# Tensor-product layer of a graph network: ScalarE scales the weights in place in PSUM, and VectorE's products read them there

## The reference, cut to what matters

```
h = silu(edge_attr @ fc_w1 * 8**-0.5)
h = silu(h @ fc_w2 * 64**-0.5)
wA, wB, wC, wD = split(h @ fc_w3 * 64**-0.5, 4)
es, ev = ys[dst], yv[dst]                 # 64 scalars, 64 x 3 vectors
sh0, sh1 = edge_sh[:, :1], edge_sh[:, 1:] # 1 and 3 numbers per edge
m0a = wA * es * sh0
m0b = wD * einsum('eud,ed->eu', ev, sh1) / sqrt(3)
m1a = wB[:, :, None] * es[:, :, None] * sh1[:, None, :]
m1b = wC[:, :, None] * ev * sh0[:, :, None]
ns, nv = segment_sum(concat(m0a, m0b), src), segment_sum(concat(m1a, m1b), src)
```

## Time and profile before

| | |
|---|---|
| Time of 3 runs | 9382.79, 9408.56, 9411.95 us; median 9408.56 |
| Profiled execution, span from first to last instruction | 9608.8 us (its device time is not recorded apart) |
| Stretch of the tensor-product layer's edge loop | from about 4396 to 5876 us |
| Busy in that stretch of 1480 us | PE 1424.10, DVE 1297.62, POOL 1179.54, ACT 451.01 us |
| TensorE's granted clock in that stretch | 0.99 of full speed |

### The profile page before, as it was taken

One profiled execution on the slowest core, in us unless ns is written; L12 is line 12 of the kernel. 1 busy time (PEld: TensorE's weight loads), 2 busy tenths in 40 slices (PEclk: granted clock), 3 DMA queues, 4 the chain that ended last, 5 costly groups with the idle time before them and its releaser, 6 DMA issues. The chain is left out here.

```text
span 9608.8 us, 121761 instructions
## 1 busy us (share of the span) xinstructions
PE 6035.1 (63%) x27004; PEld 3698.3 (38%) x27227; DVE 5624.6 (59%) x14481; ACT 2416.0 (25%) x7255; POOL 5956.5 (62%) x5564
## 2 busy tenths in 40 slices
PE   2121155555555555547999997899999997554544
PEld 0010033333333333334444444555555555333333
DVE  4100055555555555556888887899999998222224
ACT  0000033333333333322333332344444443000000
POOL 5777655555555555546888884566666665666663
PEclk6555566666666666668999998999999999667676
DMA  1000032223222232322332333344444444333334
GB/s 64 1 10 10 17 88 83 83 78 83 81 80 80 81 83 78 81 55 73 85 84 85 84 84 52 111 120 119 119 119 121 120 119 101 90 90 89 89 90 55
DMA packets 405871, 777.59 MB, mean 81 GB/s; under 512 B 195938, under 2 KB 225356, under 8 KB 405196
## 3 DMA queue, kind: packets, MB, share of 16 engines
q0 software_dynamic: 279488, 712.60, 28.4%
q1 hardware_dynamic: 126348, 64.59, 2.3%
HBM read 736.75 MB, written 40.07 MB: 81 GB/s over the span
## 5 line engine op out<-in xcount | busy, mean ns | idle before, releaser
L495 POOL DMA_INDIRECT rec_s<-wts,rows x784 | 780.5, 995 | 1085.2 <-ACT rows L467 870.5
L1829 POOL DMA_INDIRECT gat<-y,rec_sb_s x892 | 1182.5, 1326 | 298.0 <-issue 278.8
L2098 POOL DMA_INDIRECT gat<-x,rec_sb_d x892 | 846.5, 949 | 484.5 <-issue 266.2
L965 POOL DMA_INDIRECT gat<-kv,rec_sb_d x896 | 906.7, 1012 | 334.7 <-issue 272.9
L1381 POOL DMA_INDIRECT gat<-kv,rec_sb_s x900 | 861.5, 957 | 398.5 <-issue 313.9
L2113 PE MATMUL ps<-gat,oh 128*128 128x256 f32 x1760 | 648.5, 538 | 680.2 <-DVE acc L2133 253.6
L1577 DVE TENSOR_REDUCE small<-ps 128x2 f32<-128x1024 f32 x884 | 1041.7, 1216 | 6.9 <-PE ps L1445 5.7
L434 POOL DMA_INDIRECT rec_d<-small x784 | 810.7, 1034 | 343.0 <-issue 265.1
L1870 PE MATMUL ps<-big,oh 128*128 128x512 f32 x1760 | 947.3, 637 | 0.0
L2113 PEld LDWEIGHTS ps<-gat,oh 128*128 128x128 f32 x1760 | 462.9, 274 | 865.5 <-issue 497.1
L1048 PE MATMUL ps<-big,oh 128*128 128x264 f32 x1768 | 754.1, 541 | 0.3
(11 more groups left out here) (276 smaller groups left out, 13129.7 us busy)
## 6 DMA issues: line engine op xcount, KB each, us to landing
gat<-kv,rec_sb_s POOLq DMA_INDIRECT x900
gat<-kv,rec_sb_d POOLq DMA_INDIRECT x896
rec_sb_s<-rec_s SPq DMA_DIRECT2D x448, 32.0 KB, 2.2
gat<-y,rec_sb_s POOLq DMA_INDIRECT x892
gat<-x,rec_sb_d POOLq DMA_INDIRECT x892
rec_d<-small POOLq DMA_INDIRECT x784
rec_s<-wts,rows POOLq DMA_INDIRECT x784
rec_s<-gat SPq DMA_DIRECT2D x4, 1808.0 KB, 16.7
```

The lines of the kernel that those rows point to most:

```text
L495: e.indirect_dma_start(out=recs["s"], out_offset=bass.IndirectOffsetOnAxis(ap=pr[:, t:t + 1], axis=0), in_=rr[:, t, :], in_offset=None).th ...
L965: e.indirect_dma_start(out=gat[:, m.u, q, :], out_offset=None, in_=table, in_offset=bass.IndirectOffsetOnAxis(ap=r_sb[:, m.u, q, 0:1].bitc ...
L1829: e.indirect_dma_start(out=rows_y[m.u][:, q, :], out_offset=None, in_=y1, in_offset=bass.IndirectOffsetOnAxis(ap=r_sb[:, m.u, q, 0:1].bitc ...
L2098: e.indirect_dma_start(out=gat[:, m.u, q, 0:D], out_offset=None, in_=x3, in_offset=bass.IndirectOffsetOnAxis(ap=r_sb[:, m.u, q, 0:1].bitca ...
```

## The change

The tile `wac`, in which ACT put the scaled `wA` and `wC`, was a piece of the SBUF tile `work`. It is now another name for the places of `wA` and `wC` in `psW` itself. ACT's four activations read and write the same addresses in PSUM, and DVE's L1941 and L1942 take their weights from PSUM in place of SBUF. No semaphore, no count and no order of instructions is changed on any engine.

```diff
             h2 = work[:, 384:640]
-            wac = work[:, 1536:2048].rearrange("p (q a n) -> p q a n", q=Q, a=2)
             wb = work[:, 2048:2304].rearrange("p (q n) -> p q n", q=Q)
...
             psW = ps[:, 3:5, :].rearrange("p b c -> p (b c)").rearrange("p (q k n) -> p q k n", q=Q, k=4)
+            wac = psW[:, :, 0:3:2, :]
...
                 for q in range(Q):
-                    last = A.activation(wac[:, q], psW[:, q, 0:3:2, :], ACT.Copy, scale=r_sb[:, m.u, q, 2:3])
+                    last = A.activation(wac[:, q], wac[:, q], ACT.Copy, scale=r_sb[:, m.u, q, 2:3])
                 last.then_inc(s["wac"], 1)
```

## The result

The changed kernel takes 9513.67 us (9465.77 to 9523.55, four runs) against 9409.03 us (9382.79 to 9411.95, four runs) beside it: ratio 1.0105, 95% interval 1.0073 to 1.0137. The forecast was 9408 us, 9375 to 9442: the result lies 106 us above the one and 72 us above the top of the other, on the side that had a chance of 0.09.

A forecast was written before the change was run, and what follows sets the result against it. The prediction took PE to set the edge loop's 6.60-us turn, waiting each turn for ACT's L1898 behind the four L1908. ACT 0, DVE 0 and waits 0 left the 9408.56 us median unchanged: forecast 9408 us, range 9375 to 9442.

The forecast's parts named there:

- PE waits for ACT's chain, which sets the turn: Edge loop: PE waits 0.24 to 0.34 us before L1844 for L1898, queued behind four L1908; turn 6.60 us.
- ACT: duration may change, pitch won't: ACT's four L1908 a turn: pitch change 0, bounded by -35 and +107 ns; a changed duration costs nothing.
- The faster rival: L1908: writing to PSUM takes some 35 ns off ACT's pitch, 31 us less, 9378 us; chance 0.10.
- the bank rival: L1908: reading and writing one bank in turn raises the pitch; 9440 us at 35 ns, 9503 at 107; chance 0.08.
- DVE: nothing: L1941 and L1942 with one PSUM source: 0 to -2 ns each; 0.66 us idle before L1953 as cover.
- The 65 ns more for a PSUM source: L1941 and L1942 by the skill's fixed cost: 0.13 us a turn for the two, under DVE's idle time.
- Sum. ACT 0, DVE 0, waits 0.: Whole kernel: all terms add to a difference of 0, forecast 9408 us; no change had chance 0.80.
- Others reading PSUM meanwhile: L1942 reads banks 3 and 4 for 0.95 us while PE and ACT use other banks; no cost claimed.
- The rivals: Three alternatives to no change: faster pitch 0.10, bank read and written in turn 0.08, DVE becoming late 0.02.

The follow-up runs named there:

- b2: Kernel before plus a fifth 128-column ACT activation, read by nobody, ahead of the four L1908 each turn: 8547.27 us, ratio 1.0057.
- b3: Kernel before with the next macro's copy L1898 moved ahead of the four L1908 in ACT's queue: 8495.53 us, ratio 0.9998.
- e2: Changed kernel plus a GpSimd memset of 1408 unread columns after the second gather issue, same chip as e1: 9642.30 us, ratio 0.9995 against the kernel before.
- e1: Changed kernel again, beside e2 on one chip with late signals: 9766.87 us, ratio 1.0122 against the kernel before.
- a2: Changed kernel again, against the kernel before on a chip without late signals: 8480.17 us, ratio 0.9995.
- b1: Changed kernel once more, against the kernel before on another chip: 8493.32 us, ratio 0.9993.
- c1: Changed kernel a fourth time, against the kernel before on a chip where signals come late: 9521.69 us, ratio 1.0119.
- a1: Kernel before, unchanged, timed against itself on a chip without late signals: 8482.98 us, ratio 0.9998.
- b4: Changed kernel with the next macro's copy L1898 moved ahead of the four L1908: 8436.95 us, ratio 0.9931 against the kernel before.

## Why the prediction was wrong, step by step

- *PE waits for ACT's chain, which sets the turn.* Right: b2 shows it by 48 us more for one activation, b3 by the distance before L1844, 1.03 us for 1.28. That b3 gains no time all the same is due to a second bound close behind, GpSimd's gathers.
- *ACT: duration may change, pitch won't.* Right. The duration fell from 368 to 341 ns, the distance of 1.01 us for four stayed. The write to PSUM is quicker, as the Trainium skill says in "ScalarE: Activation LUTs", section "Step-by-step: what each stage is for"; it shortens only the part that nobody waits for. The faster rival and the bank rival both fall here.
- *DVE: nothing.* Right: L1941 went from 412 to 414 ns, L1942 from 948 to 947. The 65 ns more for a PSUM source, worked out in the prediction from the Trainium skill ("VectorE: DVE Perf Modes", section "The TRN2 errata — SBUF-src ops pay a fixed extra latency per instruction"), don't show in this form of instruction.
- *"Sum. ACT 0, DVE 0, waits 0."* This is the step that failed, in its last term: waits were put at nothing, and came to 105 us. In the loop 37 signals of TensorE come late, 91 us together, where before 4 did, 14 us. The part named *Others reading PSUM meanwhile* asks who shares the memory that the operands move to, and never who shares the one that they leave. That is GpSimd: 892 issues x (1326 - 999) ns = 292 us less work for it. The trace of before showed both halves, POOL at 1179.54 us and issues of 2.43 us among others of 0.95; I drew nothing from either. That this freed time is what brings the waits is shown by e2: with it filled again the 1.22% of e1 is gone.
- *That a freed engine costs time* I would not have forecast even then. By the profile before it was off the path, and on chips with punctual signals the term is zero (a2, b1). Where TensorE's signals come late it is worth +105 to +125 us (first comparison, c1, e1). The rivals held no case in which nothing gets slower and the kernel does.

Open is why TensorE's signals come late on those chips at all, and why drift brings them. Being inside an issue when the signal is due is not it: in the trace of before GpSimd is inside one at the end of 219 of 222 L1859, and the signals are on time; after, at 53 of 222. The traces of those chips record under half of the DMA signals (33150 before, about 95000 in a1), so I can't follow it further. Whether that loss of records and the late signals have one cause, no run here tells.

## What to carry to other kernels

When an operand moves from SBUF to PSUM, ask what shares the memory it leaves: VectorE's products of two SBUF tensors hold up GpSimd's gather issues, and one PSUM source frees them, which pays only where GpSimd is the next bound (b3 against b4). Before trusting a change of 1%, run it on more than one chip, and compare medians of the turn with the count of long turns: the same median with more long turns is no matter of work per turn. In that case, filling an idle engine's time can be worth more than what it costs, as in e2 against e1.

## What the runs showed of the hardware that I had not expected

- The kernel before takes 8484 and 8499 us on two chips and 9409 to 9642 in the four other comparisons. VectorE's 32 instructions of L355 have the same duration on both kinds (1026 and 1027 ns) and wait 158.5 against 5.6 us for TensorE. In the edge loop the one difference that I found is signals from TensorE that arrive up to 7 us late, followed by matmuls at half clock. How much of the whole 11 to 14% they make up wasn't counted.
- A gather issue of 0.95 us becomes 2.43 us when it starts inside a row of VectorE products with two SBUF sources; it ends 0.82 us after the row (median of 220).
- A memset of 1290 ns, 223 times, on an engine off the path made the kernel 1.3% faster than without it (e2 against e1).
